# ScalarE takes the logarithms and exponentials of a two-branch attention over four key tiles instead of two, and the weighted sums follow eight steps behind the scores

## The chip, the cores and the metric

The kernel runs on one core of one Trainium2 chip. The metric is the device time of one execution in microseconds (us). The median of three runs of the kernel before is 2053.55 us (2052.15 to 2053.83).

## What is computed

Two transformer blocks of residual layers over x of 4 x 1024 x 128. The change lies in the first layer, an attention with 16 heads of width 8 in each of 4 batches, so 64 heads of 1024 queries and 1024 keys. Each score S is weighed in two ways, and both weighted sums of V are averaged:

```python
S = jnp.einsum('bhnd,bhmd->bhnm', Q, K) / dh ** 0.5
W_tau = jax.nn.softmax(S, axis=-1)
W_sigma = 1.0 / ((1.0 + jnp.abs(S) / b_) ** 2 + t_ ** 2)
W_sigma = W_sigma / W_sigma.sum(axis=-1, keepdims=True)
...
f = 0.5 * tau + 0.5 * sigma
```

An expert layer, a causal attention and a tree layer follow. The change does not touch them.

## The kernel before

The attention is the function `attend_heads`. A head's 1024 keys are cut into 8 tiles of 128 keys; a tile of weights has 128 keys in its partitions and 1024 queries in its columns. The work is pipelined by hand: every engine runs its own `stage(s)` once per head s, with eight steps j = 0 to 7, and semaphores join the engines. Each engine issues its instructions in the written order, so an instruction that waits holds up all that stands behind it on its engine. `stages` unrolls three heads, loops over further ones and unrolls the last.

For the **sigma** weights of head s, tile j:

- TensorE (PE) writes the scores in two halves of 512 queries into the PSUM tile `ps_sig`, one buffer for each half (`sigma_scores`, L617).
- VectorE (DVE) takes each half's magnitude into the ring `sig` (`magnitude`, L718) and updates the running maximum over keys (L725, for the first tile the copy L722). The next scores of that half wait for the latter (`run_ready`).
- GpSimd (POOL) adds beta (`grow`, L833) and squares (L860), for all tiles but tile 2, which ScalarE squares (`square_whole`, L773).
- ScalarE (ACT) takes the logarithm over a chunk of `CHUNK` = 2 tiles at a time (`take_logs`, L766), and then the exponential of minus that (`invert`, L779), which gives the reciprocal. `LOG_LAG` and `EXP_LAG` say how many steps after a chunk's first tile these are issued.

For the **tau** weights, the softmax, PE turns the running maximum of head s into rows of the query operand (`turn_running` L572, `turn_maxima` L577; DVE L661; ACT L796; a DMA). The scores with that maximum taken off are then computed once more (L635, `tau_tile`) into `ps_tau`, which has two buffers, and ACT exponentiates them out of PSUM into the ring `tau` (L807). A tile of these comes with every step, four steps and a head behind.

Both kinds of weights are summed by PE in `weigh` (L604): four matmuls for a step, two halves of each kind, accumulated in `ps_acc` over the eight tiles. A step of `weigh` stands at the end of PE's step, behind both halves of the sigma scores and the tau scores. It runs `PV_LAG` = 7 steps behind the sigma scores of its tile. At the end of a head DVE copies the sums (`take_sums`, L703), PE turns them (`turn_sums`, L584) and DVE divides (L683 to L698).

So a step of PE reads: scores of half 0, tau scores, scores of half 1, `weigh`. At step 0 `turn_running` stands twice beside these, the second time behind `weigh`, and at step 1 `turn_maxima` stands behind `weigh`. A step of ACT reads: tau exponential, then whichever of square, exponential and logarithm belongs to the step.

Of the kernel before, what the change touches and what calls it, by code (L numbers as in the profile page):

```python
# [41 lines left out]
SLOTS = 3  # L42
# [2 lines left out]
GROWN_RING = 3  # L45
WHOLE = 2
POOLED = TB - 1
CHUNK = 2
SIG_RING = 12
LOG_LAG, EXP_LAG = 5, 6  # L50
PV_LAG = 7
MT_STEP, FT_STEP = 1, 3
SUMS_STEP = 7
LOOPS = (NH - 1) // SLOTS - 1
COLS = DH + 1
PAIRS = [(kind, half) for kind in range(2) for half in range(2)]
# [395 lines left out]
def attend_heads(nc, a, w):  # L452
# [14 lines left out]
    with ExitStack() as ctx:  # L467
# [62 lines left out]
        def at(s, low, high):  # L530

            return not known(s) or low <= s <= high
# [32 lines left out]
        @block.tensor  # L565
        def _(pe):
            def turn_running(slot, half, before):

                wait(pe, misc_done, before)
                for t in range(4):  # L570
                    q = half * HALF + t * P
                    mm = pe.transpose(ps_misc[:, t * P:(t + 1) * P], run[:, slot, q:q + P], w["ident"][:, :])  # L572
                mm.then_inc(misc_ready, 1)

            def turn_maxima(before):
                pe.wait_ge(misc_done, before)
                pe.transpose(ps_misc[0:TB, 0:P], rowmax[:, :], w["ident"][:, :]).then_inc(misc_ready, 1)  # L577

            def turn_sums(v, before):

                pe.wait_ge(sums_ready, v + 1)
                pe.wait_ge(misc_done, before)
                for t in range(4):
                    mm = pe.transpose(ps_misc[:, t * P:(t + 1) * P], sums[:, t * P:(t + 1) * P], w["ident"][:, :])  # L584
                mm.then_inc(misc_ready, 1)

            def weigh(v, slot, j):

                if j == 0:
                    wait(pe, sums_ready, v)  # L590
                    if at(v, 0, NH - 1):
                        pe.wait_ge(head_copied, v * 2 + 2)
                kinds = []
                if at(v, 1, NH):
                    pe.wait_ge(tau_done, v * TB + (j - TB + 1))
                    kinds.append(0)
                if at(v, 0, NH - 1):
                    pe.wait_ge(sig_done, v * (TB // CHUNK) + (j // CHUNK + 1))
                    kinds.append(1)
                for q, (kind, half) in enumerate(PAIRS):  # L600
                    if kind in kinds:
                        tile = slot * TB + j
                        weights = tau[:, (tile - TB) % TAU_RING] if kind == 0 else sig[:, tile % SIG_RING]
                        mm = pe.matmul(ps_acc[32 * q:32 * q + COLS, :], vop[:, (slot - 1 + kind) % SLOTS, j, :],  # L604
                                       weights[:, half * HALF:(half + 1) * HALF],
                                       start=(j == 0), stop=(j == TB - 1))
                mm.then_inc(pv_done, 1)

            def stage(s, slot, turn):
                before = misc_before(s)  # L610
                for j in range(TB):
                    keys = slice(j * P, (j + 1) * P)

                    def sigma_scores(half):

                        wait(pe, run_ready, s * (2 * TB) + (2 * j - 1 + half))
                        pe.matmul(ps_sig[:, half, :], kop[0:SIGMA_ROWS, slot, keys],  # L617
                                  qop[0:SIGMA_ROWS, slot, half * HALF:(half + 1) * HALF],
                                  start=True, stop=True).then_inc(sig_ready, 1)

                    if at(s, 0, NH - 1):
                        if j == 0:
                            pe.wait_ge(ops_loaded[slot], turn * LOADED + LOADED)
                        sigma_scores(0)
                    elif j == 0 and at(s, NH, NH):
                        pe.wait_ge(run_ready, 2 * TB * NH)
                    if j == 0 and at(s, 1, NH):
                        turn_running((slot - 1) % SLOTS, 0, before)
                    if tile := tau_tile(s, slot, j):
                        head, head_slot, of, g = tile  # L630
                        if of == 0:
                            pe.wait_ge(mrow_loaded, head * 32 + 32)
                        wait(pe, tau_done, g - 1)
                        for half in range(2):
                            mm = pe.matmul(ps_tau[:, of % 2, half, :], kop[:, head_slot, of * P:(of + 1) * P],  # L635
                                           qop[:, head_slot, half * HALF:(half + 1) * HALF], start=True, stop=True)
                        mm.then_inc(tau_ready, 1)
                    if at(s, 0, NH - 1):
                        sigma_scores(1)
                    if j < PV_LAG:  # L640
                        if at(s, 1, NH + 1):
                            weigh(s - 1, (slot - 1) % SLOTS, j - PV_LAG + TB)
                    elif at(s, 0, NH):
                        weigh(s, slot, j - PV_LAG)
                    if at(s, 1, NH):
                        if j == 0:
                            turn_running((slot - 1) % SLOTS, 1, before + 1)
                        if j == MT_STEP:
                            turn_maxima(before + 2)
                    if j == FT_STEP and at(s, 2, NH + 1):  # L650
                        turn_sums(s - 2, before + (3 if at(s, 0, NH) else 0))

            stages(pe, stage)
            turn_sums(NH, misc_before(NH + 1) + 1)

        @block.vector
        def _(dve):
# [47 lines left out]
            def stage(s, slot, turn):  # L705
                before = misc_before(s)
                for j in range(TB):
                    tile = slot * TB + j
                    if j == SUMS_STEP and at(s, 1, NH + 1):
                        wait(dve, misc_done, misc_before(s) if at(s, 2, NH + 1) else 0)  # L710
                        take_sums(s - 1)

                    def magnitude(half):
                        dve.wait_ge(sig_ready, s * (2 * TB) + (2 * j + half + 1))
                        if half == 0:
                            wait(dve, pv_done, s * TB + (j - SIG_RING + 1))
                        cols = slice(half * HALF, (half + 1) * HALF)
                        dve.tensor_scalar(sig[:, tile % SIG_RING, cols].bitcast(I32),  # L718
                                          ps_sig[:, half, :].bitcast(I32), SIGN_OFF, None, ALU.bitwise_and)\
                           .then_inc(mag_ready, 1)  # L720
                        if j == 0:
                            dve.tensor_copy(run[:, slot, cols], ps_sig[:, half, :]).then_inc(run_ready, 1)  # L722
                        else:
                            dve.wait_ge(run_ready, s * (2 * TB) + (2 * j - 1 + half))
                            dve.tensor_tensor(run[:, slot, cols], ps_sig[:, half, :], run[:, slot, cols], ALU.max)\  # L725
                               .then_inc(run_ready, 1)

                    if at(s, 0, NH - 1):
                        magnitude(0)
                    if j == 0 and at(s, 1, NH):  # L730
                        half_maxima(0, before)
                    sums_use = before + (3 if at(s, 0, NH) else 0)
                    if j == FT_STEP + 1 and at(s, 2, NH + 1):
                        invert(s - 2, sums_use)
                    if j == FT_STEP + 2 and at(s, 2, NH + 1):
                        complete(s - 2, sums_use)
                    if at(s, 0, NH - 1):
                        magnitude(1)
                    if at(s, 1, NH):
                        if j == 0:  # L740
                            half_maxima(1, before + 1)
                        if j == MT_STEP + 1:
                            second_part(s - 1)
                    if j == FT_STEP + 1 and at(s, 2, NH + 1):
                        divide(s - 2)

            dve.memset(ps_acc[:, :], 0.0).then_inc(acc_set, 1)
            stages(dve, stage)
# [5 lines left out]
        def _(act):  # L754
# [43 lines left out]
            def stage(s, slot, turn):  # L798
                for j in range(TB):
                    if j == MT_STEP + 1 and at(s, 1, NH):  # L800
                        first_part(s - 1, misc_before(s) + 2)
                    if tile := tau_tile(s, slot, j):
# [4 lines left out]
                        act.activation(tau[:, (head_slot * TB + of) % TAU_RING, :],  # L807
                                       ps_tau[:, of % 2, :, :].rearrange("p h q -> p (h q)"),
                                       ACT.Exp, scale=float(DH) ** -0.5).then_inc(tau_done, 1)
                    if j == WHOLE + LOG_LAG - 1 and at(s, 0, NH - 1):  # L810
                        square_whole(s, slot)
                    lagged(invert, s, slot, j, EXP_LAG)
                    lagged(take_logs, s, slot, j, LOG_LAG)
# [765 lines left out]
```

## Time and profile before

| | us |
|---|---|
| profiled execution, device time | 2050.47 |
| its span, first to last instruction | 2048.6 |
| median of the three runs | 2053.55 |
| PE busy in the span | 1571.4 (77%) |
| DVE busy | 1800.0 (88%) |
| ACT busy | 1634.4 (80%) |
| POOL busy | 1419.3 (69%) |

The busy times are those of the whole span. In the page's row of 40 slices ACT and DVE stand at 9 tenths or more from the fourth slice to about the thirtieth, which is the attention, and far lower before and behind it. Shares of the span thus say less than a look at the attention by itself: a stretch from its middle, the time from one instruction of a head to the same one of the next head, and what each engine waits for in between. Records of ACT and DVE overlap a little, since the next instruction starts before the last one has ended; what an instruction costs an engine that never waits is the time from its start to the next start.

### The profile page before, as it was taken

To read this page: it belongs to the slowest core of one execution; us is meant where nothing else is said; L and a number is where in the kernel's file an instruction comes from. 1 tells how busy PE (TensorE), PEld (TensorE's weight loads), DVE (VectorE), ACT (ScalarE), POOL (GpSimd) and SP (SyncE) were. 2 spreads that over 40 slices of the span, in tenths; PEclk is the share of its full clock that TensorE was granted. 3 is DMA by queue.
4 is the path that set the end of the run, shared out by engine and by line. 5 is a ranking of instruction groups with operands and counts; after the bars stand their busy time and mean duration, and the time that the engine had idled before them with its cause. 6 is when DMAs were issued, how large, how long until landed. Compare 5 with 4: busy or idle time off the path is not lost. (4 is left out here: it accounts for less than half of the span.)

```text
span 2048.6 us, 33898 instructions
## 1 busy us (share of the span) xinstructions
PE 1571.4 (77%) x8452; PEld 572.2 (28%) x8579; DVE 1800.0 (88%) x3699; ACT 1634.4 (80%) x1459; POOL 1419.3 (69%) x1070
## 2 busy tenths in 40 slices
PE   4477777877777777777777778777777587788866
PEld 2212222222222222222222222222221243366655
DVE  5799999999999999999999999999998288755556
ACT  3279999999999999999999999999999311222243
POOL 1398999889998899988999899998998112000010
PEclk9689999999999999999999999999999788877878
DMA  3300000000000000000000000000000000000001
GB/s 106 110 4 15 12 12 12 15 14 12 12 12 15 14 12 12 12 15 14 12 12 13 16 12 12 12 13 16 12 12 6 1 1 0 1 0 0 0 1 41
DMA packets 28862, 31.74 MB, mean 15 GB/s; under 512 B 5209, under 2 KB 16544, under 8 KB 28832
## 3 DMA queue, kind: packets, MB, share of 16 engines
q1 hardware_dynamic: 28832, 31.40, 5.0%
q8 instruction: 12, 0.20, 0.0%
q14 instruction: 18, 0.15, 0.0%
HBM read 22.74 MB, written 8.39 MB: 15 GB/s over the span
## 5 line engine op out<-in xcount | busy, mean ns | idle before, releaser
L860 POOL TENSOR_TENSOR sigma_weights<-grown 128x1024 f32<-128x1024 f32 x448 | 845.7, 1894 | 0.0
L718 DVE TENSOR_SCALAR sigma_weights<-ps_sig 128x512 int32<-128x512 int32 x1024 | 693.2, 677 | 26.5 <-PE ps_sig L617 26.5
L604 PE MATMUL ps_acc<-tau_weights,v_operand 128*9 128x512 f32 x2048 | 529.5, 596 | 134.3 <-ACT sigma_weights L779 134.0
L725 DVE TENSOR_TENSOR running_max<-ps_sig,running_max 128x512 f32<-128x512 f32 x896 | 608.2, 679 | 0.0
L833 POOL TENSOR_SCALAR grown<-sigma_weights,shape_operand 128x1024 f32<-128x1024 f32 x448 | 501.7, 1120 | 139.9 <-DVE sigma_weights L718 139.9
L617 PE MATMUL ps_sig<-q_operand,k_operand 96*128 96x512 bf16 x1024 | 400.2, 391 | 180.3 <-DVE running_max L725 165.2
L604 PE MATMUL ps_acc<-sigma_weights,v_operand 128*9 128x512 f32 x2048 | 531.4, 597 | 0.1
L766 ACT ACTIVATE sigma_weights<-sigma_weights,shape_operand 128x2048 f32<-128x2048 f32 x256 | 508.6, 1987 | 11.2 <-POOL sigma_weights L860 11.2
L807 ACT ACTIVATE tau_weights<-ps_tau 128x1024 f32<-128x1024 f32 x512 | 510.8, 998 | 8.0 <-PE ps_tau L635 8.0
L779 ACT ACTIVATE sigma_weights<-sigma_weights 128x2048 f32<-128x2048 f32 x256 | 484.6, 1893 | 0.0
L635 PE MATMUL ps_tau<-q_operand,k_operand 128*128 128x512 bf16 x897 | 277.8, 379 | 7.9 <-DMA q_operand<-max_rows 0.4
L617 PEld LDWEIGHTS ps_sig<-q_operand,k_operand 96*128 96x128 bf16 x1024 | 98.3, 96 | 658.5 <-DVE running_max L725 595.2
L604 PEld LDWEIGHTS ps_acc<-tau_weights,v_operand 128*9 128x9 f32 x2048 | 54.6, 88 | 296.0 <-ACT sigma_weights L779 192.6
L635 PEld LDWEIGHTS ps_tau<-q_operand,k_operand 128*128 128x128 bf16 x1024 | 100.0, 98 | 58.9 <-issue 4.3
L1317 POOL TENSOR_TENSOR x_res<-x_res,bo_rows 128x512 f32 x8 | 9.9, 1263 | 153.2 <-DVE z_c L1207 153.2
L572 PE MATMUL ps_misc<-ident,running_max 128*128 128x128 f32 x512 | 81.0, 280 | 14.2 <-DVE row_max L661 13.3
L661 DVE TENSOR_REDUCE row_max<-ps_misc 128x4 f32<-128x512 f32 x128 | 87.4, 683 | 2.4 <-PE ps_misc L572 2.4
L1023 PE MATMUL ps_me<-experts,turned_sb 128*128 128x512 f32 x128 | 73.7, 727 | 20.1 <-DVE x_res L1136 19.8
L722 DVE COPY running_max<-ps_sig 128x512 f32<-128x512 f32 x128 | 87.4, 683 | 0.0
L1510 POOL TENSOR_TENSOR x_res<-x_res,bout_rows 128x512 f32 x8 | 10.0, 1265 | 104.3 <-DVE z_d L1451 104.3
L696 DVE TENSOR_TENSOR f_heads<-f_heads,quotient 128x64 f32 (+1 forms) x64 | 81.4, 1272 | 0.1
L572 PEld LDWEIGHTS ps_misc<-ident,running_max 128*128 128x128 f32 x512 | 59.1, 141 | 79.7 <-DVE row_max L661 73.1
(172 smaller groups left out, 1511.5 us busy)
## 6 DMA issues: line engine op xcount, KB each, us to landing
q_operand<-q_parts SPq DMA_DIRECT2D x192, 48.0 KB
k_operand<-k_parts SPq DMA_DIRECT2D x64, 144.0 KB
q_parts<-parts SPq DMA_DIRECT2D x12, 256.0 KB, 2.9
k_parts<-parts SPq DMA_DIRECT2D x12, 256.0 KB, 2.9
x_res<-in_L_attn_x SPq DMA_DIRECT2D x4, 512.0 KB, 7.0
q_operand<-max_rows SPq DMA_DIRECT2D x128, 2.0 KB
out<-x_res SPq DMA_DIRECT2D x4, 512.0 KB, 3.2
experts<-in_L_ffn_expert_w SPq DMA_DIRECT2D x1, 512.0 KB
```

The costliest lines, as they stand in the source:

```text
L572: mm = pe.transpose(ps_misc[:, t * P:(t + 1) * P], run[:, slot, q:q + P], w["ident"][:, :])
L604: mm = pe.matmul(ps_acc[32 * q:32 * q + COLS, :], vop[:, (slot - 1 + kind) % SLOTS, j, :], weights[:, half * HALF:(half + 1) * HALF], star ...
L617: pe.matmul(ps_sig[:, half, :], kop[0:SIGMA_ROWS, slot, keys], qop[0:SIGMA_ROWS, slot, half * HALF:(half + 1) * HALF], start=True, stop=Tr ...
L635: mm = pe.matmul(ps_tau[:, of % 2, half, :], kop[:, head_slot, of * P:(of + 1) * P], qop[:, head_slot, half * HALF:(half + 1) * HALF], sta ...
L661: dve.tensor_reduce(rowmax[:, 4 * half:4 * half + 4], ps_misc[:, :].rearrange("p (t k) -> p t k", t=4), AX.X, ALU.max).then_inc(misc_done, 1)
L718: dve.tensor_scalar(sig[:, tile % SIG_RING, cols].bitcast(I32), ps_sig[:, half, :].bitcast(I32), SIGN_OFF, None, ALU.bitwise_and)\
L725: dve.tensor_tensor(run[:, slot, cols], ps_sig[:, half, :], run[:, slot, cols], ALU.max)\
L766: act.activation(tile, tile, ACT.Ln, bias=shape[:, slot, 1:2]).then_inc(ln_done, 1)
L779: act.activation(tile, tile, ACT.Exp, scale=-1.0).then_inc(sig_done, 1)
L807: act.activation(tau[:, (head_slot * TB + of) % TAU_RING, :], ps_tau[:, of % 2, :, :].rearrange("p h q -> p (h q)"), ACT.Exp, scale=float( ...
L833: pool.tensor_scalar(grown[:, tile % GROWN_RING, :], u, 1.0, shape[:, slot, 0:1], ALU.mult, ALU.add)\
L860: pool.tensor_tensor(sig[:, tile % SIG_RING, :], t, t, ALU.mult)\
```

## The change

`CHUNK` goes from 2 to 4, so that ACT takes two logarithms and two exponentials per head over 128 x 4096 elements, where it took four of each over 128 x 2048. The lags follow: logarithms stand at step 6 (tiles 0 to 3) and at step 2 of the next head (tiles 4 to 7), exponentials at step 7 and at step 3, always behind the tau exponential of that step. ACT's square of tile 2 moves from step 6 to step 5. `weigh` runs eight steps behind the scores instead of seven, so that step j of head s sums tile j of the sigma weights of head s - 1. DVE's copy of the finished sums moves from the beginning of step 7 to its end.

```diff
-CHUNK = 2
+CHUNK = 4
 SIG_RING = 12
-LOG_LAG, EXP_LAG = 5, 6
-PV_LAG = 7
+SQUARE_LAG, LOG_LAG, EXP_LAG = 3, 6, 7
 MT_STEP, FT_STEP = 1, 3
-SUMS_STEP = 7
...
-                    if j < PV_LAG:
-                        if at(s, 1, NH + 1):
-                            weigh(s - 1, (slot - 1) % SLOTS, j - PV_LAG + TB)
-                    elif at(s, 0, NH):
-                        weigh(s, slot, j - PV_LAG)
+                    if at(s, 1, NH + 1):
+                        weigh(s - 1, (slot - 1) % SLOTS, j)
...
-                    if j == SUMS_STEP and at(s, 1, NH + 1):
-                        wait(dve, misc_done, misc_before(s) if at(s, 2, NH + 1) else 0)
-                        take_sums(s - 1)
-
...
+                    if j == TB - 1 and at(s, 1, NH + 1):
+                        wait(dve, misc_done, misc_before(s) if at(s, 2, NH + 1) else 0)
+                        take_sums(s - 1)
...
-                    if j == WHOLE + LOG_LAG - 1 and at(s, 0, NH - 1):
+                    if j == WHOLE + SQUARE_LAG and at(s, 0, NH - 1):
                         square_whole(s, slot)
```

How ACT's instructions stood before, from step 0 to step 4 of a head in the loop (`tau_weights` is the tau exponential of a step, `sigma_weights<-sigma_weights` alone the exponential over a chunk, with `shape_operand` the logarithm):

```order
L807 ACTIVATE tau_weights<-ps_tau 128x1024
...
L779 ACTIVATE sigma_weights<-sigma_weights 128x2048
...
L807 ACTIVATE tau_weights<-ps_tau 128x1024
...
L766 ACTIVATE sigma_weights<-sigma_weights,shape_operand 128x2048
...
L796 ACTIVATE max_rows<-ps_misc 8x128
...
L807 ACTIVATE tau_weights<-ps_tau 128x1024
...
L779 ACTIVATE sigma_weights<-sigma_weights 128x2048
...
L807 ACTIVATE tau_weights<-ps_tau 128x1024
...
L766 ACTIVATE sigma_weights<-sigma_weights,shape_operand 128x2048
...
L807 ACTIVATE tau_weights<-ps_tau 128x1024
```

And now, for the same steps 0 to 4 (line numbers are those of the changed kernel: L801 is the tau exponential, L760 the logarithm, L773 the exponential over a chunk, L790 the copy of the maxima):

```order
L801 ACTIVATE tau_weights<-ps_tau 128x1024
...
L801 ACTIVATE tau_weights<-ps_tau 128x1024
...
L790 ACTIVATE max_rows<-ps_misc 8x128
...
L801 ACTIVATE tau_weights<-ps_tau 128x1024
...
L760 ACTIVATE sigma_weights<-sigma_weights,shape_operand 128x4096
...
L801 ACTIVATE tau_weights<-ps_tau 128x1024
...
L773 ACTIVATE sigma_weights<-sigma_weights 128x4096
...
L801 ACTIVATE tau_weights<-ps_tau 128x1024
```

Steps 0, 1 and 4 have lost their chunk's work, and steps 2 and 3 hold twice as much each; steps 4 to 7 repeat this with the square at step 5.

On PE the place is the end of step 0 in the loop, with the semaphores that each row waits for. Before:

```order
L617 MATMUL ps_sig<-q_operand,k_operand 128x512 [waits running_max_ready]
L595 ISA
L598 ISA [waits tau_weights_ready]
L604 MATMUL ps_acc<-tau_weights,v_operand 9x512 [waits sigma_weights_ready]
L604 MATMUL ps_acc<-tau_weights,v_operand 9x512
L604 MATMUL ps_acc<-sigma_weights,v_operand 9x512 x2
L130 REGISTER_ALU
L572 MATMUL ps_misc<-ident,running_max 128x128 [waits misc_read]
```

And now (L615 are the scores, L602 is `weigh`, L570 `turn_running`):

```order
L615 MATMUL ps_sig<-q_operand,k_operand 128x512 [waits running_max_ready]
L128 REGISTER_ALU
L590 ISA [waits sums_ready]
L593 ISA [waits head_copied]
L596 REGISTER_ALU [waits tau_weights_ready]
L602 MATMUL ps_acc<-tau_weights,v_operand 9x512 [waits sigma_weights_ready]
L602 MATMUL ps_acc<-tau_weights,v_operand 9x512
L602 MATMUL ps_acc<-sigma_weights,v_operand 9x512 x2
L128 REGISTER_ALU
L570 MATMUL ps_misc<-ident,running_max 128x128 [waits misc_read]
```

The first tile of a head is now weighed at step 0 of the next head, where it was weighed at step 7 of its own, and it still waits for the exponential of its chunk ahead of the second `turn_running`.

## Rows read from the trace of the kernel before

**Rows 1.** Stretches: us; busy by engine, PE, PEld, DVE, ACT, POOL; granted clock; DMA.

```profile
300.00:1500.00 1200.00, 948.15 (x5541) 257.78 (x5644) 1179.18 (x2071) 1200.00 (x932) 1088.76 (x829) 1.00 0.04 13
```

**Rows 2.** Timeline of ACT: start, duration, line, operation; from one square to the next.

```profile
808.23 1.13 ACT L773 ACTIVATE sigma_weights<-sigma_weights,shape_operand 128x1024 f32<-128x1024 f32 x1
809.27 1.89 ACT L779 ACTIVATE sigma_weights<-sigma_weights 128x2048 f32<-128x2048 f32 x1
811.07 1.00 ACT L807 ACTIVATE tau_weights<-ps_tau 128x1024 f32<-128x1024 f32 x1
811.98 1.99 ACT L766 ACTIVATE sigma_weights<-sigma_weights,shape_operand 128x2048 f32<-128x2048 f32 x1
813.87 1.00 ACT L807 ACTIVATE tau_weights<-ps_tau 128x1024 f32<-128x1024 f32 x1
...
831.43 1.13 ACT L773 ACTIVATE sigma_weights<-sigma_weights,shape_operand 128x1024 f32<-128x1024 f32 x1
```

**Rows 3.** Timeline of DVE, same head; in brackets idle time before and its releaser.

```profile
806.97 0.68 DVE L725 TENSOR_TENSOR running_max<-ps_sig,running_max 128x512 f32<-128x512 f32 x1
...
824.36 0.69 DVE L718 TENSOR_SCALAR sigma_weights<-ps_sig 128x512 int32<-128x512 int32 x1 [0.40 <-PE ps_sig L617]
824.97 0.68 DVE L725 TENSOR_TENSOR running_max<-ps_sig,running_max 128x512 f32<-128x512 f32 x1
```

**Rows 4.** Timeline of PE, same head: `weigh`, scores, `turn_running`, `turn_maxima`, tau scores.

```profile
807.70 0.39 PE L617 MATMUL ps_sig<-q_operand,k_operand 96*128 96x512 bf16 x1 [1.22 <-DVE running_max L725]
...
811.22 0.60 PE L604 MATMUL ps_acc<-tau_weights,v_operand 128*9 128x512 f32 x2 [0.73 <-ACT sigma_weights L779]
...
812.20 0.39 PE L617 MATMUL ps_sig<-q_operand,k_operand 96*128 96x512 bf16 x1
...
812.86 0.59 PE L635 MATMUL ps_tau<-q_operand,k_operand 128*128 128x512 bf16 x2
813.29 0.38 PE L617 MATMUL ps_sig<-q_operand,k_operand 96*128 96x512 bf16 x1
813.60 0.60 PE L604 MATMUL ps_acc<-tau_weights,v_operand 128*9 128x512 f32 x2
...
814.87 0.66 PE L572 MATMUL ps_misc<-ident,running_max 128*128 128x128 f32 x4 [0.23 <-DVE row_max L661]
815.37 0.38 PE L617 MATMUL ps_sig<-q_operand,k_operand 96*128 96x512 bf16 x1
...
817.70 0.27 PE L577 MATMUL ps_misc<-ident,row_max 128*8 128x128 f32 x1
817.86 0.39 PE L617 MATMUL ps_sig<-q_operand,k_operand 96*128 96x512 bf16 x1
818.09 0.60 PE L635 MATMUL ps_tau<-q_operand,k_operand 128*128 128x512 bf16 x2
...
823.85 0.38 PE L617 MATMUL ps_sig<-q_operand,k_operand 96*128 96x512 bf16 x1
...
824.81 0.60 PE L604 MATMUL ps_acc<-tau_weights,v_operand 128*9 128x512 f32 x2
```

**Rows 5.** Timeline of POOL, same head: the square of tile 7.

```profile
817.24 1.91 POOL L860 TENSOR_TENSOR sigma_weights<-grown 128x1024 f32<-128x1024 f32 x1
```

**Rows 6.** Timeline of PE where the attention drains, behind the last head's scores.

```profile
1588.53 0.60 PE L604 MATMUL ps_acc<-tau_weights,v_operand 128*9 128x512 f32 x2 [2.46 <-ACT sigma_weights L779]
...
1594.03 0.70 PE L604 MATMUL ps_acc<-tau_weights,v_operand 128*9 128x512 f32 x2 [1.92 <-ACT sigma_weights L779]
```

**Rows 7.** Stretches of 1 us behind the second of these waits, columns as in rows 1.

```profile
1594.00:1595.00 1.00, 0.97 (x8) 0.14 (x8) 0.00 (x0) 0.79 (x1) 0.00 (x0) 0.70 0.00 0
1595.00:1596.00 1.00, 0.67 (x5) 0.13 (x2) 0.00 (x0) 0.00 (x0) 0.00 (x0) 0.50 0.06 16
1596.00:1597.00 1.00, 1.00 (x5) 0.13 (x8) 0.00 (x0) 0.39 (x1) 0.00 (x0) 0.50 0.00 0
1597.00:1598.00 1.00, 1.00 (x8) 0.00 (x0) 0.00 (x0) 0.64 (x1) 0.00 (x0) 0.59 0.00 0
```

## The prediction

> **What bounds the kernel now.** I read the stretches first, because shares of the whole span mix the attention with the layers behind it. In 1200 us from the middle of the attention ACT is busy for all 1200 us, DVE for 1179 us, POOL for 1089 us and PE for 948 us at a granted clock of 1.00, which is 2.4 GHz [rows 1]. Then ACT's timeline, where one square marks a head: 808.23 to 831.43, so 23.20 us a head [rows 2]. ACT starts each instruction right as the last one ends and never waits: it sets the pace. DVE comes close behind. Its only wait in that head is 0.40 us for scores [rows 3], so without ACT it could not go below 22.80 us. PE waits for both, at most 1.22 us at a time [rows 4]. The reader should keep two things apart: how much work ACT has per head, and where in the eight steps it lies. The change lowers the first and alters the second.
>
> **ACT's work.** From start to start a tau exponential takes 0.91 us, a logarithm over 2048 columns 1.89, an exponential over 2048 columns 1.80 and a square over 1024 columns 1.04 [rows 2]. Square and logarithm both take a bias column and both go from SBUF to SBUF, so 1024 columns more cost 1.89 - 1.04 = 0.85 us, and a logarithm's fixed share is about 0.19 us; an exponential's is 1.80 - 1.70 = 0.10 us. A logarithm over 4096 columns is an estimate of 1.89 + 2 x 0.85 = 3.59 us. An exponential, whose whole duration over 2048 columns is 1.89 us [rows 2], is 1.89 + 1.70 = 3.59 us to its end. Two of each fall away per head: 2 x 0.19 + 2 x 0.10 = 0.58 us. ACT's work goes from 23.20 to 22.62 us. That is the gain, if nothing else moves.
>
> **Where it lies.** By the order printed above, ACT now has tau, logarithm, tau, exponential in steps 2 and 3, and again in steps 6 and 7. It can't start this earlier, since each tau exponential waits for the tau scores of its own step, and PE computes those only in step 2 (or 6), between scores that DVE must have freed. And `weigh` of step 4 (or of step 0 of the next head) waits for the end of that exponential. From ready tau scores to the start of `weigh` this takes 0.91 + 3.59 + 0.91 + 3.59 us and 0.06 us for the signal, which is what lay between the end of an exponential (809.27 + 1.89 = 811.16, [rows 2]) and the `weigh` behind it (811.22, [rows 4]): **9.06 us**. Before, the tau scores of step 2 began at 818.09 and ended 0.60 later, and `weigh` of step 4 began at 824.81 [rows 4]: 6.1 us for the same path. So PE will now stand before `weigh` for about 3 us, twice per head. Behind `weigh` on PE stand the next scores of half 0, the next tau scores and, at step 0, `turn_running`. DVE's next magnitudes wait for the former, so DVE stops, and ACT's tau exponential of the step after next waits too. The exponential releases PE, PE releases ACT: a loop through both engines, walked twice per head.
>
> **The loop, added up** from `weigh` back to ready tau scores. After `weigh` of step 4: `weigh` 0.98 us (811.22 to 812.20), scores to tau scores 0.23 (817.86 to 818.09), tau scores to the other scores 0.43 (812.86 to 813.29), to `weigh` 0.31 (813.29 to 813.60), `weigh` again 0.98, scores of step 6 0.23, its tau scores 0.59 to their end, signal 0.06 [rows 4]: 3.81 us. After `weigh` of step 0: 0.98, then `turn_running` of 0.66, 0.13 until DVE starts (823.85 + 0.38 to 824.36), its maximum and a magnitude at 0.60 each (824.36 to 824.97), then 0.73 from the start of the running maximum to the scores that it releases (806.97 to 807.70) [rows 3, 4]: 3.70 us to the scores of step 2. PE's own road there (0.98 + 0.50 + 0.23 + 0.43 + 0.31 + 0.98 + 0.16 = 3.59, with 814.87 to 815.37 and 817.70 to 817.86 [rows 4]) is no longer. With 0.23 + 0.59 + 0.06 that is 4.58 us. The head takes 3.81 + 9.06 + 4.58 + 9.06 = **26.51 us**, 3.31 more than before. Stages 1 to 63 have both kinds of work, so 63 x 3.31 = 208.5 us.
>
> The other edits I cost at nothing. The square at step 5 lies between two tau exponentials where ACT now waits. DVE's copy of the sums, at the end of step 7 instead of its beginning, lies beside PE's wait. POOL's square of tile 7, which the logarithm of step 2 needs, ends at 817.24 + 1.91 = 819.15 [rows 5], and the tau exponential ahead of that logarithm could not end before 818.09 + 0.60 + 0.91 = 819.60 [rows 4]; with DVE stopped POOL gains further room. If that cover went, the logarithm would start by the difference later. The first wait and the last drain change by a microsecond or so. **Bounds** of the unknown price: 6.8 us (eight times 0.85, no fixed share at all) to 7.56 us (4 x 1.89) for a logarithm and an exponential where I take 7.18; over 126 such pairs this is about 48 us to either side.
>
> **The clock.** PE now waits about 3 us where it waited 1.22 at most. The attention's drain has the same sort of wait: PE stood before `weigh` for 2.46 us at 1588.53 and for 1.92 us at 1594.03 [rows 6], and just behind the second the granted clock fell to 0.50, half speed, and came back within four slices: 0.30 + 0.50 + 0.50 + 0.41 = 1.71 us of clock lost [rows 7]. The first of the two left no such fall. The Trainium skill's page "TensorE: Matmul & The Clock Gate" (Part 1: The HAM clock gate) says that half rate is the default and activity alone lifts it; rows 6 and 7 agree, and by that rule waits like these cost more than their own length. Behind `weigh` the loop is almost all PE's, so a fall there delays the next tau scores by what is lost. The bounds are 0 and 1.71 us per wait. I take 1.6, near the upper, because the new waits are longer than the one that was followed by a fall; a fall that begins in the wait itself spends a part there. That is 3.2 us per head, 63 x 3.2 = 201.6 us.
>
> **Sum.** 2050.47 (the profiled execution, span 2048.6) + 208.5 + 201.6 = 2460.6 us. The median of the runs is 3.1 us above that execution, so 2464 us.
>
> **Rivals.**
> - *The waits come, the clock stays at 1.00.* For it: no fall behind the 2.46 us wait [rows 6]. 2053.6 + 208.5 = 2262 us.
> - *It falls at one of the two waits of a head*, or at every other one: 2262 + 101 = 2363 us.
> - *Faster: the exponentials are in time.* ACT's 0.58 us come off until DVE's 22.80 us bound, 63 x 0.40 = 25 us: 2028 us. It decides at the point where tau, logarithm, tau and exponential take no longer than the 6.1 us that PE and DVE need from the tau scores of step 2 to `weigh` of step 4, or where a tau exponential can run ahead of its step. The first would need half the columns; the second speaks against PE's order. The Trainium skill's page "ScalarE: Activation LUTs" (What ACT_TABLE_LOAD costs) gives 186 ns of fixed cost per ACTIVATE, 93 ns more with a pointer as bias, and an overlap of 93 ns with the next. By it four instructions less would save 2 x 186 + 2 x 93 = 558 ns per head, and rows 2 agree with 0.58 us. It is a rule of the sum of work and says nothing of the loop.
> - *No change:* the slack between steps swallows just the wait. Nothing in the rows speaks for it.
> - *The clock stays low throughout:* PE's parts of the loop double, 2 x 3.81 + 2 x 4.58 + 18.12 = 34.9 us, near 2790 us. Against it: behind the drain's fall it came back while PE was busy [rows 7].
> - *A smaller slowdown*, 2100 to 2225 us, if part of PE's road overlaps with ACT's in a way that I don't see.
>
> That the change doesn't do what it says can't be: the printed order shows two logarithms and two exponentials per head.
>
> **Chances.** Waits with a fall at nearly each 0.48; without falls 0.22; with half of them 0.12; faster 0.07; no change 0.03; clock low throughout 0.04; a smaller slowdown 0.04. About 0.2%, 4 us, is what a measurement of this kernel can tell from no change. So faster 0.07, same 0.03, slower 0.90. The range holds the first three cases with the bounds of ACT's price: 2262 - 37 = 2225 below, 2464 + 46 = 2510 above. The forecast's own range is 2400 to 2510.
>
> **What would show it.** Right: a head near 29.7 us, ACT with 7 us idle per head ahead of tau exponentials (steps 0, 1, 4 to 6), PE's longest waits about 3 us before `weigh`, released by the exponential, DVE's waits for scores twice per head, POOL idle more, and stretches of PE clock at 0.50. A head of 26.5 us with a clock of 1.00 would keep the loop and refute the clock. Logarithms and exponentials near 3.6 us show ACT's price. Wrong: ACT busy all through the attention, or a head under 23.2 us.

## The result, and the profile after

The changed kernel takes 2525.58 us (median of four runs, 2523.99 to 2527.2), where the kernel before took 2052.85 us beside it (2051.61 to 2053.83): a ratio of 1.2312, with a 95% interval of 1.2297 to 1.2327. The forecast was slower, 2464 us, with a range up to 2510 us. The way was right; the time lies 62 us above the forecast and 16 us above the range.

First the stretch from 300 to 1500 us of the changed kernel, to be read against [rows 1]: us; busy by engine, PE, PEld, DVE, ACT, POOL; granted clock; DMA.

```profile
300.00:1500.00 1200.00, 861.10 (x4259) 216.41 (x4261) 855.51 (x1564) 903.65 (x547) 823.32 (x624) 0.83 0.03 10
```

No engine is busy throughout any more. ACT, which was busy for all of these 1200 us, now works for 904; DVE fell from 1179 to 856 us, PE's clock from 1.00 to 0.83. Where every engine has idle time, the chain of waits sets the pace, and the list of waits of that stretch names it (who waited for whom: us in total, times, longest):

```profile
PE ps_acc L602 <- ACT sigma_weights L773: 315.3, 78, 4.1
...
ACT tau_weights L801 <- PE ps_tau L633: 254.7, 118, 3.5
...
DVE sigma_weights L709 <- PE ps_sig L615: 195.3, 78, 4.4
...
DVE row_max L656 <- PE ps_misc L570: 153.0, 40, 3.8
```

In the order of the causes: PE stands before `weigh` until ACT's exponential is done, 78 times in 39 heads, so twice per head, up to 4.1 us. DVE then waits for the scores that stand behind `weigh` on PE, or at step 0 for `turn_running`, which stands there too. And ACT waits for the tau scores that stand behind those. ACT's timeline shows one head between two squares, 808.95 to 839.67:

```profile
804.43 1.02 ACT L801 ACTIVATE tau_weights<-ps_tau 128x1024 f32<-128x1024 f32 x1
808.03 1.03 ACT L801 ACTIVATE tau_weights<-ps_tau 128x1024 f32<-128x1024 f32 x1 [2.58 <-PE ps_tau L633]
808.95 1.14 ACT L767 ACTIVATE sigma_weights<-sigma_weights,shape_operand 128x1024 f32<-128x1024 f32 x1
809.99 1.02 ACT L801 ACTIVATE tau_weights<-ps_tau 128x1024 f32<-128x1024 f32 x1
810.90 3.70 ACT L760 ACTIVATE sigma_weights<-sigma_weights,shape_operand 128x4096 f32<-128x4096 f32 x1
814.50 1.01 ACT L801 ACTIVATE tau_weights<-ps_tau 128x1024 f32<-128x1024 f32 x1
815.41 3.62 ACT L773 ACTIVATE sigma_weights<-sigma_weights 128x4096 f32<-128x4096 f32 x1
...
823.41 1.02 ACT L801 ACTIVATE tau_weights<-ps_tau 128x1024 f32<-128x1024 f32 x1 [3.48 <-PE ps_tau L633]
...
826.21 1.03 ACT L801 ACTIVATE tau_weights<-ps_tau 128x1024 f32<-128x1024 f32 x1 [0.38 <-PE ps_tau L633]
...
839.67 1.14 ACT L767 ACTIVATE sigma_weights<-sigma_weights,shape_operand 128x1024 f32<-128x1024 f32 x1
```

That is 30.72 us per head, against 23.20 [rows 2]. The long instructions themselves are as cheap as forecast: from start to start a logarithm takes 814.50 - 810.90 = 3.60 us, and an exponential is done after 3.62 us. PE's timeline shows the two waits, and the first scores behind each:

```profile
804.68 1.03 PE L602 MATMUL ps_acc<-tau_weights,v_operand 128*9 128x512 f32 x2 [4.10 <-ACT sigma_weights L773]
...
806.51 0.61 PE L615 MATMUL ps_sig<-q_operand,k_operand 96*128 96x512 bf16 x1
...
819.07 1.03 PE L602 MATMUL ps_acc<-tau_weights,v_operand 128*9 128x512 f32 x2 [3.98 <-ACT sigma_weights L773]
...
835.40 1.03 PE L602 MATMUL ps_acc<-tau_weights,v_operand 128*9 128x512 f32 x2 [4.10 <-ACT sigma_weights L773]
```

`weigh` of step 4 lasts 1.83 us from 804.68 to the next scores, where it took 0.98 us [rows 4]. The slices of 1 us show why; the clock is the third column from the end:

```profile
804.00:805.00 1.00, 0.32 (x4) 0.16 (x8) 0.00 (x0) 1.00 (x2) 1.00 (x1) 0.66 0.19 76
805.00:806.00 1.00, 1.00 (x8) 0.00 (x0) 0.00 (x0) 0.45 (x1) 0.25 (x1) 0.50 0.17 66
...
807.00:808.00 1.00, 1.00 (x4) 0.21 (x2) 0.76 (x2) 0.00 (x0) 0.00 (x0) 0.63 0.00 0
...
817.00:818.00 1.00, 0.00 (x0) 0.00 (x0) 1.00 (x3) 1.00 (x1) 1.00 (x1) 0.99 0.00 0
818.00:819.00 1.00, 0.00 (x0) 0.00 (x0) 0.23 (x1) 1.00 (x2) 1.00 (x2) 0.50 0.00 0
...
824.00:825.00 1.00, 1.00 (x8) 0.00 (x0) 1.00 (x2) 0.44 (x1) 0.16 (x1) 0.60 0.00 0
```

Behind the wait of step 4 the clock is at half speed from 804.3 to 807.7 and 0.34 + 0.50 + 0.50 + 0.37 = 1.71 us of clock are lost, as in [rows 7]. Behind the wait of step 0 it is at half speed in all six slices from 818 to 824, and 0.01 + 6 x 0.50 + 0.40 = 3.41 us are lost, twice as much. All 39 heads of this stretch show both: a fall of 3.4 us behind the one wait and of 6.8 us behind the other.

### The profile page after: what moved, and what is told of

It is laid out like the page before. It is cut to its first block and busy times, and to the rows that moved or that the text cites. A ratio compares the mean times of both kernels' runs of the same rounds, so it can differ in the third digit from the quotient of the medians.

```text
span 2522.1 us, 33548 instructions
## 1 busy us (share of the span) xinstructions
PE 1805.6 (72%) x8579; PEld 607.7 (24%) x8579; DVE 1742.9 (69%) x3699; ACT 1630.6 (65%) x1203; POOL 1423.4 (56%) x1070
## 3 DMA queue, kind: packets, MB, share of 16 engines
HBM read 22.74 MB, written 8.39 MB: 12 GB/s over the span
## 5 line engine op out<-in xcount | busy, mean ns | idle before, releaser
L602 PE MATMUL ps_acc<-tau_weights,v_operand 128*9 128x512 f32 x2048 | 670.3, 741 | 510.7 <-ACT sigma_weights L773 510.3
L801 ACT ACTIVATE tau_weights<-ps_tau 128x1024 f32<-128x1024 f32 x512 | 522.7, 1021 | 409.3 <-PE ps_tau L633 409.3
L602 PE MATMUL ps_acc<-sigma_weights,v_operand 128*9 128x512 f32 x2048 | 671.2, 742 | 2.9 <-ACT sigma_weights L773 2.9
L615 PE MATMUL ps_sig<-q_operand,k_operand 96*128 96x512 bf16 x1024 | 444.0, 434 | 62.2 <-DVE running_max L716 44.0
L760 ACT ACTIVATE sigma_weights<-sigma_weights,shape_operand 128x4096 f32<-128x4096 f32 x128 | 473.8, 3702 | 6.0 <-POOL sigma_weights L854 6.0
L773 ACT ACTIVATE sigma_weights<-sigma_weights 128x4096 f32<-128x4096 f32 x128 | 462.8, 3616 | 0.1
L633 PE MATMUL ps_tau<-q_operand,k_operand 128*128 128x512 bf16 x1024 | 360.5, 438 | 0.2 <-DMA q_operand<-max_rows 0.2
L615 PEld LDWEIGHTS ps_sig<-q_operand,k_operand 96*128 96x128 bf16 x1024 | 109.0, 107 | 577.5 <-DVE running_max L716 409.9
L602 PEld LDWEIGHTS ps_acc<-tau_weights,v_operand 128*9 128x9 f32 x2048 | 58.0, 90 | 709.6 <-issue 450.3
L570 PE MATMUL ps_misc<-ident,running_max 128*128 128x128 f32 x512 | 110.4, 355 | 1.0 <-DVE running_max L716 1.0
L570 PEld LDWEIGHTS ps_misc<-ident,running_max 128*128 128x128 f32 x512 | 78.2, 179 | 115.5 <-issue 108.9
L767 ACT ACTIVATE sigma_weights<-sigma_weights,shape_operand 128x1024 f32<-128x1024 f32 x64 | 72.9, 1139 | 7.0 <-POOL sigma_weights L854 7.0
L1130 DVE SCALAR_TENSOR_TENSOR x_res<-ps_me,gate_weight,x_res 128x128 f32 (+1 forms) x256 | 68.2, 341 | 6.8 <-PE ps_me L1017 5.2
```

The lines of the kernel that those rows point to most:

```text
L760: act.activation(tile, tile, ACT.Ln, bias=shape[:, slot, 1:2]).then_inc(ln_done, 1)
L773: act.activation(tile, tile, ACT.Exp, scale=-1.0).then_inc(sig_done, 1)
```

## The experiments

Two theories stood against each other at first: that the work's place in the steps makes a loop of ScalarE and TensorE, which TensorE's clock then lengthens (mine), and that the later weighted sums, or the long instruction by itself, cost the time. All times are compared with runs of the kernel before on the same chip (medians 2050.19, 2050.88 and 2051.77 us in the three groups of runs below).

### The two halves of the change apart

The lag alone, with chunks of two tiles as before (`e1_lag_alone`):

```diff
-CHUNK = 4
+CHUNK = 2
...
-SQUARE_LAG, LOG_LAG, EXP_LAG = 3, 6, 7
+SQUARE_LAG, LOG_LAG, EXP_LAG = 4, 5, 6
```

> Chunks of two tiles as before, with the weighted sums eight steps behind and the sums copied at the end of step 7. My theory (a loop through ScalarE's two long instructions and TensorE) expects no waits beyond those of before: ScalarE paces with 23.2 us a head, 2048 to 2058 us. Rival (the later weighted sums cost the time): most of the 470 us stays, over 2300 us.

Measured: 2048.95 us, a ratio of 0.9997 (0.9987 to 1.0007). In the stretch from 300 to 1500 us ACT is busy throughout again:

```profile
300.00:1500.00 1200.00, 991.45 (x5639) 259.86 (x5638) 1179.67 (x2070) 1200.00 (x932) 1090.11 (x829) 0.97 0.04 13
```

The eighth step and the later copy of the sums cost nothing. The rest is the chunk's. One thing in this row is new: the clock is 0.97, where it was 1.00. PE waits here up to 1.6 us for DVE, where it waited 1.2 us at most in the kernel before; no longer waits had been expected:

```profile
PE ps_sig L615 <- DVE running_max L716: 138.0, 248, 1.6
```

Behind the longest of these waits, one in each head, the clock fell to half speed for 3.4 us in 21 of 51 heads. ACT never waits here, so these falls cost no time.

Whether the chunk's size or its place matters, the next run tells: two instructions of 2048 columns back to back where one of 4096 stood (`e2_two_by_two`):

```diff
-                act.activation(tile, tile, ACT.Exp, scale=-1.0).then_inc(sig_done, 1)
+                act.activation(tile[:, 0:2, :], tile[:, 0:2, :], ACT.Exp, scale=-1.0)
+                act.activation(tile[:, 2:4, :], tile[:, 2:4, :], ACT.Exp, scale=-1.0).then_inc(sig_done, 1)
```

and the same for the logarithm.

> The changed kernel with two instructions of 2048 columns back to back in the place of each one of 4096. My theory (it is the place of the work, not the size of an instruction) expects the path of 9.1 us to grow to 9.4 us, twice per head: some 36 us more than the changed kernel, near 2560 us, give or take 60 us as the clock falls differently. Rival (one long instruction is what hurts, for itself): near the time of before, 2050 to 2100 us.

Measured: 2530.29 us, a ratio of 1.2343 (1.2318 to 1.2368). So the small instructions of before, put into these steps, are as slow as the large ones: the place is the cause. One thing came out otherwise than reckoned. ACT's road is longer (821.45 to 825.05 for the two exponentials, 9.37 us in all from the tau exponential at 815.84 to `weigh` at 825.21), yet a head takes 30.72 us, just as in the changed kernel:

```profile
783.41 1.14 ACT L768 ACTIVATE sigma_weights<-sigma_weights,shape_operand 128x1024 f32<-128x1024 f32 x1
814.13 1.14 ACT L768 ACTIVATE sigma_weights<-sigma_weights,shape_operand 128x1024 f32<-128x1024 f32 x1
```

What ACT added, the falls of the clock gave back. The two waits, and the slices at the ends of the falls behind them:

```profile
809.80 1.03 PE L602 MATMUL ps_acc<-tau_weights,v_operand 128*9 128x512 f32 x2 [3.84 <-ACT sigma_weights L775]
...
825.21 1.03 PE L602 MATMUL ps_acc<-tau_weights,v_operand 128*9 128x512 f32 x2 [4.47 <-ACT sigma_weights L775]
```

```profile
807.00:808.00 1.00, 0.00 (x0) 0.00 (x0) 1.00 (x3) 1.00 (x2) 0.35 (x1) 0.81 0.17 39
...
814.00:815.00 1.00, 1.00 (x9) 0.11 (x2) 0.99 (x2) 1.00 (x2) 0.37 (x1) 0.78 0.00 0
...
824.00:825.00 1.00, 0.00 (x0) 0.00 (x0) 0.00 (x0) 1.00 (x1) 1.00 (x2) 0.84 0.00 0
...
828.00:829.00 1.00, 1.00 (x8) 0.31 (x8) 0.81 (x2) 0.05 (x1) 0.00 (x0) 0.95 0.00 0
```

Here the long fall lies at step 4, from 807.6 to 814.4, and the short one at step 0, from 824.7 to 828.1: the other way round than in the changed kernel. Both begin earlier ahead of `weigh` than their like there (2.2 and 0.5 us, against 1.1 and 0.4), so less of them lies behind it. The time from `weigh` to the tau exponential that it lets start is 6.04 and 5.86 us, together 11.90, where the changed kernel takes 5.31 + 7.14 = 12.45 us. That is 0.55 us less, and ACT's two roads are 0.55 us longer (9.45 + 9.37 against 9.08 + 9.19).

Next ACT's road was shortened instead. In `e6_half_columns` each logarithm and exponential takes two of its four tiles, at the same place in the order; half of the sigma weights stay untransformed, so this kernel serves the timing alone:

```diff
-                act.activation(tile, tile, ACT.Exp, scale=-1.0).then_inc(sig_done, 1)
+                act.activation(tile[:, 0:2, :], tile[:, 0:2, :], ACT.Exp, scale=-1.0).then_inc(sig_done, 1)
```

> The changed kernel, but each logarithm and exponential takes only the first two of its four tiles, so half of the sigma weights stay untransformed. My theory expects the path from tau scores to the weighted sums to take 0.91 + 1.89 + 0.91 + 1.89 us, less than the 6.1 us that the other engines need, so that no long wait is left and VectorE bounds: 2015 to 2040 us. Rival (the later weighted sums cost the time): over 2300 us.

Measured: 2027.61 us, 0.9891 (0.9871 to 0.9911). The stretch:

```profile
300.00:1500.00 1200.00, 996.66 (x5733) 263.92 (x5725) 1194.20 (x2101) 872.89 (x736) 1105.31 (x841) 0.98 0.04 13
```

DVE is busy for 1194 of 1200 us and bounds. With 2048 columns the road of 5.7 us is shorter than the 6.1 us of the other engines, and nothing of the slowdown is left.

### The clock

The changed kernel with 14 more score matmuls in each of the two waits (`e3_busy_waits`), so that PE is busy while it waits:

```diff
+                    extra = {0: 14, 4: 14}.get(j, 0)
+                    if extra and tile and at(s, 2, NH - 1):
+                        pe.wait_ge(tau_done, g)
+                        for i in range(extra):
+                            pe.matmul(ps_tau[:, (of + 1) % 2, i % 2, :], kop[0:SIGMA_ROWS, slot, 0:P],
+                                      qop[0:SIGMA_ROWS, slot, 0:HALF], start=True, stop=True)
                     if at(s, 1, NH + 1):
                         weigh(s - 1, (slot - 1) % SLOTS, j)
```

> The changed kernel with 14 more score matmuls in each of TensorE's two long waits of a head, into a PSUM half that is free there; their results are overwritten and not used. My theory (3.3 us of a head are the loop, 4.2 us are the clock) expects a granted clock near 1.00, a head of 26.5 us and 2255 to 2275 us. If the clock were not what makes the rest, 2500 us or more.

Measured: 2275.59 us, 1.1101 (1.1078 to 1.1123): 0.6 us over the range that was expected, and 250 us less than the changed kernel, by more work on PE. Its stretch, two squares of ACT one head apart, and PE at the wait of step 0 (the second row's group of 14 are the added matmuls):

```profile
300.00:1500.00 1200.00, 1103.28 (x6157) 337.25 (x6155) 979.53 (x1799) 1039.97 (x631) 946.15 (x719) 1.00 0.04 11
```

```profile
801.96 1.14 ACT L773 ACTIVATE sigma_weights<-sigma_weights,shape_operand 128x1024 f32<-128x1024 f32 x1
...
828.65 1.14 ACT L773 ACTIVATE sigma_weights<-sigma_weights,shape_operand 128x1024 f32<-128x1024 f32 x1
```

```profile
808.08 0.39 PE L615 MATMUL ps_sig<-q_operand,k_operand 96*128 96x512 bf16 x1
808.58 3.19 PE L642 MATMUL ps_tau<-q_operand,k_operand 96*128 96x512 bf16 x14
812.08 0.60 PE L602 MATMUL ps_acc<-tau_weights,v_operand 128*9 128x512 f32 x2 [0.31 <-ACT sigma_weights L779]
```

The added matmuls end 0.31 us before `weigh` starts, so they hold nothing up. The clock stands at 1.00 and a head takes 26.69 us: the loop by itself, 3.49 us more than before. The other 30.72 - 26.69 = 4.03 us are the clock's. To price the two falls apart, each wait was filled alone (`e7_busy_step0` with `{0: 14}`, `e8_busy_step4` with `{4: 14}`).

> The changed kernel with the 14 more matmuls in the wait of step 0 alone. Its fall of the clock took 2.6 us a head, so my theory expects about 2525 - 63 x 2.6 = 2360 us, with one fall per head left, behind the wait of step 4. If the two falls hang together, 2275 or 2525 us.

> The changed kernel with the 14 more matmuls in the wait of step 4 alone. Its fall took 1.5 us a head and 0.1 us of signal: about 2525 - 63 x 1.6 = 2425 us, with one fall per head left, behind the wait of step 0. If the two falls hang together, 2275 or 2525 us.

Measured: 2397.81 us (1.1685, 1.1662 to 1.1709) and 2388.36 us (1.1639, 1.1616 to 1.1663). Neither number was hit: over the 2275.59 us of the run with both waits filled, one wait costs 122 us at step 4 (1.94 us a head) and 113 us at step 0 (1.79 us), where I expected 1.5 and 2.6. The falls are separate, but the place does not set their price, as the long fall at step 4 of `e2_two_by_two` shows too. The first of these two kernels shows it in two heads that follow each other, by the waits of step 4 on PE and the slices at the ends of the falls behind them:

```profile
818.17 1.03 PE L602 MATMUL ps_acc<-tau_weights,v_operand 128*9 128x512 f32 x2 [3.57 <-ACT sigma_weights L779]
...
846.21 1.03 PE L602 MATMUL ps_acc<-tau_weights,v_operand 128*9 128x512 f32 x2 [3.58 <-ACT sigma_weights L779]
```

```profile
817.00:818.00 1.00, 0.00 (x0) 0.00 (x0) 0.00 (x0) 1.00 (x2) 1.00 (x2) 0.81 0.25 47
...
821.00:822.00 1.00, 1.00 (x11) 0.12 (x8) 1.00 (x3) 0.57 (x1) 0.00 (x0) 0.99 0.00 0
...
844.00:845.00 1.00, 0.00 (x0) 0.00 (x0) 0.94 (x4) 1.00 (x1) 0.68 (x1) 0.96 0.12 45
...
851.00:852.00 1.00, 1.00 (x6) 0.20 (x3) 0.39 (x1) 0.68 (x1) 0.97 (x1) 0.63 0.00 0
```

The waits are alike (3.57 and 3.58 us), but the clock is low from 817.6 to 821.0 in the one head and from 844.9 to 851.7 in the next. In the first the fall began some 0.6 us ahead of `weigh`, in the second 1.3 us. The same holds in the changed kernel: 0.4 us ahead at step 4 (short), 1.1 us at step 0 (long). In the stretch from 300 to 1500 us the kernel with step 0 filled has 25 short falls and 17 long ones, and the one with step 4 filled has 27 and 15, so a fall costs about the same on average at either place.

### Ways out

If the loop is ACT's road against the steps that `weigh` stays behind, more steps must open it. `weigh` was put nine and ten steps behind (`e4_lag9`, `e5_lag10`; the sums are then copied at step 1 or 2 of the head after next, and a stage is added at the end). The cut of the edit with ten steps; with nine, `EXTRA` is 1:

```diff
-TAU_RING = 6
+TAU_RING = 8
...
+EXTRA = 2
...
-                    if at(s, 1, NH + 1):
-                        weigh(s - 1, (slot - 1) % SLOTS, j)
+                    if j >= EXTRA:
+                        if at(s, 1, NH + 1):
+                            weigh(s - 1, (slot - 1) % SLOTS, j - EXTRA)
+                    elif at(s, 2, NH + 2):
+                        weigh(s - 2, (slot - 2) % SLOTS, j - EXTRA + TB)
...
```

> The changed kernel with the weighted sums nine steps behind instead of eight (and a ring of eight tau tiles). My theory expects the road of the other engines from the tau scores of step 2 to the weighted sums of step 5 to be about 8.5 to 8.9 us, a little under ScalarE's 9.1 us: waits of some tenths of a us are left, no fall of the clock, 22.8 to 23.3 us a head, 2028 to 2060 us. Rival (four tiles in one instruction cost time by themselves, or the clock falls anyway): over 2200 us.

> The same with ten steps. My theory expects no wait of TensorE for the exponentials at all, VectorE as the bound with 22.8 us a head, and 2022 to 2035 us, which would be 0.8 to 1.4% faster than before. Rival (ScalarE's bursts still hold up something else, such as the tau tiles): 2050 us or more.

Measured: 2045.83 us with nine steps, 0.9979 (0.9969 to 0.9989), and 2031.27 us with ten, 0.9902 (0.9885 to 0.9918). With nine steps PE still waits for the exponential, 98 times in the stretch of 300 to 1500 us:

```profile
PE ps_acc L603 <- ACT sigma_weights L778: 127.6, 98, 1.9
```

```profile
300.00:1500.00 1200.00, 983.28 (x5676) 256.62 (x5674) 1186.28 (x2083) 1186.96 (x730) 1096.95 (x833) 0.97 0.04 13
```

The time lies in the range expected, but two details do not. These waits last 1.3 us on average, not some tenths of a us, and the clock, which was not to fall, is at half speed for 3.4 us 22 times in this stretch.

With ten steps the list of waits has no row of PE waiting for this exponential, and a head takes 22.72 to 22.74 us, a little under the 22.80 us that the prediction gave as DVE's bound:

```profile
300.00:1500.00 1200.00, 992.41 (x5722) 259.06 (x5721) 1194.00 (x2103) 1193.81 (x736) 1106.34 (x842) 0.99 0.04 13
```

```profile
838.76 1.15 ACT L772 ACTIVATE sigma_weights<-sigma_weights,shape_operand 128x1024 f32<-128x1024 f32 x1
...
861.48 1.15 ACT L772 ACTIVATE sigma_weights<-sigma_weights,shape_operand 128x1024 f32<-128x1024 f32 x1
```

DVE and ACT are both busy for 1194 of 1200 us here, so ACT has next to no room left either: its 22.62 us per head were forecast. This version beats both kernels, the one before by 1.0%. That the gain is the four tiles' and not the lag's, ten steps with two tiles show (`e10_lag10_two`, the lags of `e1_lag_alone` with `EXTRA = 2`):

> Chunks of two tiles with the sums ten steps behind, so that against the run with four tiles and ten steps only the size of ScalarE's instructions differs. My theory expects ScalarE to pace again with 23.2 us a head, 2045 to 2058 us: the longer lag alone gives nothing. Rival (the gain of the ten steps has nothing to do with four tiles): 2022 to 2035 us.

Measured: 2051.45 us, 1.0001 (0.9992 to 1.0011), with ACT busy for all 1200 us of the stretch.

The loop also runs through the order on ACT. In `e9_chunk_first` the lag stays at eight, but each logarithm and exponential stands ahead of the tau exponential of its step:

```diff
+                    lagged(invert, s, slot, j, EXP_LAG)
+                    lagged(take_logs, s, slot, j, LOG_LAG)
                     if tile := tau_tile(s, slot, j):
...
                         square_whole(s, slot)
-                    lagged(invert, s, slot, j, EXP_LAG)
-                    lagged(take_logs, s, slot, j, LOG_LAG)
```

> The changed kernel with each logarithm and exponential ahead of the tau exponential of its step instead of behind it, all else the same. If the road from ready tau scores through ScalarE is what holds TensorE (my theory), one tau exponential leaves it and the logarithm need not wait for the tau scores of its step: I work out 12.1 and 12.0 us from one wait's end to the next instead of 13.6 and 12.9, so 24 to 24.6 us a head and 2100 to 2150 us if the clock stays up, up to 2300 us if it still falls. Rival (twice the work in two steps cannot be hidden with a lag of eight, in whatever order): 2450 us or more.

Measured: 2311.01 us, 1.1269 (1.1247 to 1.1292), a little over the 2300 us expected if the clock still falls. From one wait's end to the next it takes 13.67 and 13.64 us on PE, over 12.1 and 12.0 us by 1.6 us each:

```profile
800.36 1.03 PE L602 MATMUL ps_acc<-tau_weights,v_operand 128*9 128x512 f32 x2 [2.68 <-ACT sigma_weights L773]
814.03 1.03 PE L602 MATMUL ps_acc<-tau_weights,v_operand 128*9 128x512 f32 x2 [2.19 <-ACT sigma_weights L773]
827.67 1.03 PE L602 MATMUL ps_acc<-tau_weights,v_operand 128*9 128x512 f32 x2 [2.68 <-ACT sigma_weights L773]
```

So this order takes 215 us off the changed kernel's time, and a fall still comes with each wait of 2.2 or 2.7 us, 88 times in the stretch from 300 to 1500 us: the clock there is 0.87. All 88 are of the short kind, so the loop and the falls are both smaller here, and the run does not part the two.

## Why the prediction was right and wrong

- **ACT's work: right.** 4096 columns were forecast at 3.59 us for a logarithm (3.60 measured from start to start) and 3.59 us to an exponential's end (3.62). The saving of 0.58 us per head is there; the ten-step version collects 0.48 us of it, where DVE has no room left.
- **The loop: right.** The head was added up as 3.81 + 9.06 + 4.58 + 9.06 = 26.51 us. With the clock kept up it is 26.69: from `weigh` at 812.08 the four parts take 4.55 us (to the tau exponential of step 2), 9.19 (to `weigh` of step 4), 3.87 (to the tau exponential of step 6) and 9.08 (to `weigh` of step 0). The missing 0.18 us are mostly the signal from the exponential of step 3 to `weigh`, 0.15 us where I took 0.06, and the square, which was costed at nothing and here ends 0.07 us too late for the tau exponential behind it.
- **The fall of the clock: right that it falls at each wait, wrong in its size.** The step that failed reads "The bounds are 0 and 1.71 us per wait. I take 1.6". The trace held one fall behind a wait, and its loss was taken for the most that a wait can cost. In the changed kernel the fall behind step 4 adds 5.31 - 3.81 = 1.50 us to the loop's part (`weigh` at 804.68 to the tau exponential at 809.99), but the one behind step 0 adds 7.14 - 4.58 = 2.56 us (819.07 to 826.21), because it lasts twice as long. The reason that I gave for staying under the bound, that a fall which begins in the wait spends a part of itself there, holds between falls of one length: with `e2_two_by_two` beside the changed kernel, a short fall added 1.50 us when it began 0.4 us ahead of `weigh` and 5.86 - 4.58 = 1.28 us when it began 0.5 us ahead, a long one 2.56 us from 1.1 us ahead and 6.04 - 3.81 = 2.23 us from 2.2 us ahead. What it left out is that a fall can last twice as long, and so cost more than the 1.71 us that were called a bound. With 4.06 us for both instead of 3.2, and 0.15 us of signals, a head is 30.72 us instead of 29.71; 63 x 1.0 us are the 62 us by which the time was missed. The Trainium skill's page "TensorE: Matmul & The Clock Gate" (Part 1: The HAM clock gate) lists two states of the clock, half rate and full, and the slices agree, 0.50 and 1.00.
- **The rivals.** *The waits come, the clock stays* is what 14 matmuls per wait make of the kernel, 2275.59 us where 2262 were given. *It falls at one of two waits* was put at 2363 us; with either wait filled it is 2388 to 2398. *Faster* was put at 2028 us, with the point at which it decides; with half the columns it came out at 2027.61, and with ten steps, where the road is given more time instead, at 2031.27. *The clock stays low throughout* is refuted by the stretch's clock of 0.83.
- **The range.** Its ends use 37 and 46 us for the bounds of ACT's price, where the working gave 48. With 48 the upper end is 2512 us, and the measured time still lies above it.
- **What would show it.** ACT idles 2.58 + 3.48 + 0.38 = 6.44 us per head ahead of tau exponentials, and 1.12 us ahead of the copy of the maxima, where 7 us were forecast. PE's longest waits were forecast at 3 us and are 4. More than half of that miss is not the clock's: with the clock kept up in `e3_busy_waits`, from the end of the last scores (808.08 + 0.39) to `weigh` at 812.08 is 3.61 us already. So the other engines' road from tau scores to `weigh`, taken as 6.1 us, is nearer 5.5 us in this loop; the sum of the loop did not use it.

Left open: what decides at which moment of a wait the clock falls. Among the falls behind the long waits for ACT in the stretch from 300 to 1500 us (the changed kernel, `e2_two_by_two`, `e7_busy_step0`, `e8_busy_step4` and `e9_chunk_first`), every one of 3.4 us began at most 0.58 us ahead of `weigh`, some of them only behind its start, and every one of 6.8 us began at least 0.68 us ahead. That is what the traces show side by side; no run set that moment on purpose, so it is not shown to be the cause.

## What to carry to other kernels

Batching two instructions into one saves their fixed cost but delivers the first half later: where engines hand work round in a circle, add up the road from the first input to the last output of the larger batch, and give the consumer as many steps of lag as that takes. Here 0.58 us saved per head cost 7.5 us with a lag of eight steps and gained 0.5 us with ten. And a wait of TensorE is not priced by its length alone: look for what its clock did behind the nearest waits of the same kind, and don't take a single such fall for the worst.

## What the runs showed of the hardware that was not expected

- More work made the kernel 250 us faster: 28 matmuls per head in TensorE's waits kept the granted clock at 1.00 (2525.58 against 2275.59 us).
- A fall of the clock behind a wait lasted either 3.4 or 6.8 us and lost about 1.7 or 3.4 us of clock, for waits of the same length (3.57 and 3.58 us in `e7_busy_step0`). Of the two waits of a head the long fall was at step 0 in the changed kernel and at step 4 in `e2_two_by_two`.
- A wait of 1.62 us was followed by a fall in 21 of 51 heads of `e1_lag_alone`, one of 1.22 us in none of 51 heads of the kernel before. Length alone does not decide it, since the wait of 2.46 us in [rows 6] left no fall.
- With falls at both waits a head's time does not follow the work: with ACT's two roads of a head at 18.27 us in all and at 18.82 us it is 30.72 us alike. Without falls, 0.55 us more per head would be the estimate from these roads.
- VectorE's addition of 128 x 64 elements, `f_heads<-f_heads,quotient`, takes 1.32 us in the kernel before at 805.12, beside a multiplication of GpSimd that lasts until 806.36; the addition ends at 806.44. It takes 0.21 us in the changed kernel at 808.45, where GpSimd is idle (from 805.25 to 809.50). It is off the loop there and gains nothing.
